# Norm scalars of a batch: the one-column operations on ScalarE instead of VectorE

## The reference

```python
m, s = mean and variance of x over each of 32 groups (4 channels, all pixels)
g = (x - m) / sqrt(s + 1e-5)                      # group norm
u, v = mean and variance (ddof=1) of g over the 128 channels of one pixel
n = (g - u) / (sqrt(v) + 1e-6)                    # per pixel
out = g + g * (W @ n + b)                         # W: 128 x 128, over channels
```

## Time and profile before

| | |
|---|---|
| median of the runs | 1894.35 us (1892.35 to 1896.38) |
| the profiled execution: its own time, its span | 1890.62 us, 1888.8 us |
| mean granted clock of TensorE over the span | 0.996 |
| instructions in the span | 67606 |
| HBM read, written | 394.49 MB, 268.44 MB |
| DMA, mean over the span | 353 GB/s |

### The profile page before, as it was taken

One profiled execution on the slowest core, in us unless ns is written; L12 is line 12 of the kernel. 1 busy time (PEld: TensorE's weight loads), 2 busy tenths in 40 slices (PEclk: granted clock), 3 DMA queues, 4 the chain that ended last, 5 costly groups with the idle time before them and its releaser, 6 DMA issues.

```text
span 1888.8 us, 67606 instructions
## 1 busy us (share of the span) xinstructions
PE 1699.3 (90%) x28706; PEld 920.7 (49%) x28706; DVE 1727.5 (91%) x2120; ACT 1446.4 (77%) x2498; POOL 1458.4 (77%) x1684
## 2 busy tenths in 40 slices
PE   0079998999989999999999999899999999899998
PEld 0045554555545555455555555455545555455553
DVE  5669999999999999999999999999999999988887
ACT  5589886888868986798869889688877898644442
POOL 0068787888878887888878787787877888788885
PEclk9989999999999999999999999999999999999999
DMA  9979999999999999999999999899999999854775
GB/s 375 407 285 375 375 373 327 390 394 391 364 339 406 375 396 342 344 407 382 383 323 393 400 386 381 314 402 386 397 349 340 416 373 397 290 205 189 276 264 221
DMA packets 183036, 667.33 MB, mean 353 GB/s; under 512 B 20560, under 2 KB 20944, under 8 KB 182736
## 3 DMA queue, kind: packets, MB, share of 16 engines
q1 hardware_dynamic: 109008, 394.54, 56.9%
q10 hardware_dynamic: 73728, 268.47, 35.4%
HBM read 394.49 MB, written 268.44 MB: 351 GB/s over the span
## 4 chain that ended last, share of the span: by engine, by line
PE 68%; DVE 18%; issue 6%; DMA 3%; SPq 2%; ACT 2%; POOL 1%; POOLq 0%; ACTq 0%; DVEq 0%
PE proj_ps L731 40%; PE sums_ps L719 15%; PE factor_ps L705 12%; DVE scaled L629 5%; DVE bn L673 4%; DVE bn L674 4%; DMA tiles<-x 3%; SPq L410 2%; DVE tiles L642 1%; DMA out<-tiles 1%; DVE gn L583 1%; ACT unused L511 1%; ACT squares L526 0%; DVE gn L587 0%; POOL tiles L454 0%
## 5 line engine op out<-in xcount | busy, mean ns | idle before, releaser
L731 PE MATMUL proj_ps<-scaled,w_t 128*32 128x512 f32 x8192 | 985.9, 599 | 0.1
L454 POOL TENSOR_SCALAR tiles<-tiles,columns_sb 128x1024 f32<-128x1024 f32 x512 | 576.9, 1127 | 257.4 <-DVE tiles L642 254.4
L642 DVE SCALAR_TENSOR_TENSOR tiles<-proj_ps,columns_sb,tiles 128x1024 f32<-128x1024 f32 x512 | 643.3, 1257 | 69.1 <-PE proj_ps L731 67.5
L511 ACT ACTIVATE unused<-tiles,bn 128x1024 uint8<-128x1024 f32 x560 | 635.2, 1134 | 0.0
L443 POOL TENSOR_SCALAR tiles<-tiles,columns_sb 128x1024 f32<-128x1024 f32 x512 | 620.4, 1212 | 12.9 <-DMA tiles<-x 11.7
L629 DVE TENSOR_TENSOR scaled<-tiles,factor_ps 128x1024 f32<-128x1024 f32 x512 | 619.0, 1209 | 7.2 <-PE factor_ps L705 2.1
L526 ACT ACTIVATE squares<-tiles 128x1024 f32<-128x1024 f32 x512 | 537.8, 1050 | 81.3 <-POOL tiles L443 37.0
L719 PEld LDWEIGHTS sums_ps<-tiles,const_sb 128*32 128x32 f32 x8192 | 245.8, 111 | 316.3 <-issue 265.2
L731 PEld LDWEIGHTS proj_ps<-scaled,w_t 128*32 128x32 f32 x8192 | 213.6, 109 | 360.8 <-issue 306.8
L705 PE MATMUL factor_ps<-pieces,pick_sb 128*128 128x128 bf16 x4096 | 318.1, 221 | 77.2 <-DVE scaled L629 72.5
L719 PE MATMUL sums_ps<-tiles,const_sb 128*32 128x128 f32 x8192 | 320.6, 275 | 11.7 <-ACT squares L526 11.7
(11 more groups left out here) (56 smaller groups left out, 782.3 us busy)
## 6 DMA issues: line engine op xcount, KB each, us to landing
tiles<-x SPq DMA_DIRECT2D x752, 512.0 KB, 8.6
out<-tiles ACTq DMA_DIRECT2D x512, 512.0 KB, 7.1
const_sb<-const SPq DMA_DIRECT2D x1, 85.5 KB, 1.9
scaled<-w SPq DMA_DIRECT2D x1, 64.0 KB, 2.0
scaled<-ident SPq DMA_DIRECT2D x1, 64.0 KB, 1.8
pick_sb<-pick SPq DMA_DIRECT2D x1, 8.0 KB, 2.0
columns_sb<-bias SPq DMA_DIRECT2D x1, 0.5 KB, 2.1
```

Of the source, the lines that this page charges most:

```text
L454: nc.gpsimd.tensor_scalar(place(s), place(s), 1.0, out_shift[:, 0:1], ALU.mult, ALU.add).then_inc(finished, 1)
L511: nc.scalar.activation(unused[:, which, :], data, (ACT.Identity, ACT.Square)[which], bias=pivot_of(of), scale=-1.0, accum_out=act_sums[:, ...
L642: nc.vector.scalar_tensor_tensor(out=place(s), in0=proj_ps[:, s % 2, :], scalar=gate_shift[:, 0:1], in1=place(s), op0=ALU.add, op1=ALU.mul ...
L731: mm = nc.tensor.matmul(proj_ps[q:q + 32, s % 2, h:h + BANK], w_t[:, q:q + 32], scaled[:, s % 2, h:h + BANK], start=True, stop=True)
```

## The change

The `bn_aggr` and the sum of ACT's statistics stay on DVE (`gather`), one step earlier, in step 58. So do the two reciprocals (`invert_root`, `invert_std`). The other small instructions become ACT instructions: eight in `moments` at the end of ACT's step 59, two in `deviation` at the end of step 61, eight in `spread_of_group` in step 62, right behind the square of the slot and ahead of the set work (the pieces of L536 and L539). Each waits for the one before it on `gn_step`, and the sixteenth waits for DVE's reciprocal of the root. PE's two averages stay in steps 61 and 62 (GN_STEP is now 58). DVE's `invert_root` stands in step 62 behind scale, where the clamp stood, and `invert_std` behind the gate of step 62. POOL's wait for slot 0 is for all 18 steps and for `inv_std_done`; the gate of a batch's first slot gets a wait on `gn_step`, which lies nine steps behind. A constant column holds 1e-5.

```diff
-        GN_STEPS = 19
-        GN_STEP = slots - 5
+        GN_STEPS = 18
+        GN_STEP = slots - 6
...
+            def moments(n, of):
+                total = slots * SLOT
+                bn_part = of.bn_slots / slots
+                act.wait_ge(gn_gathered, 2 * n + 2)
+                gn_then(nc.scalar.activation(cell(4), cell(0), ACT.Identity, bias=pivot_of(of), scale=-1.0), n, 1)
+                gn_then(nc.scalar.activation(cell(5), cell(4), ACT.Identity, bias=cell(1), scale=cell(4)), n, 2)
+                gn_then(nc.scalar.activation(cell(6, 2), cell(2, 2), ACT.Copy, scale=1.0 / total), n, 3)
+                gn_then(nc.scalar.activation(cell(8), cell(4), ACT.Identity, bias=cell(6), scale=bn_part), n, 4)
+                gn_then(nc.scalar.activation(cell(9), cell(5), ACT.Identity, bias=cell(7), scale=bn_part), n, 5)
+                gn_then(nc.scalar.activation(cell(10), cell(8), ACT.Copy, scale=-1.0), n, 6)
+                gn_then(nc.scalar.activation(cell(11), cell(8), ACT.Identity, bias=pivot_of(of), scale=-1.0), n, 7)
+                gn_then(nc.scalar.activation(cell(4), cell(8), ACT.Identity, bias=cell(9), scale=cell(10)), n, 8)
+
+            def deviation(n):
+                act.wait_ge(group_mean_done, n + 1)
+                gn_then(nc.scalar.activation(cell(5), small_ps[:, 0:1], ACT.Identity, bias=cell(11), scale=-1.0), n, 9)
+                gn_then(nc.scalar.activation(cell(12), cell(5), ACT.Identity, bias=cell(4), scale=cell(5)), n, 10)
+
+            def spread_of_group(n):
+                act.wait_ge(group_var_done, n + 1)
+                gn_then(nc.scalar.activation(cell(8), small_ps[:, 1:2], ACT.Relu), n, 11)
+                gn_then(nc.scalar.add(cell(9), cell(8), at["gn_eps"]), n, 12)
+                gn_then(nc.scalar.activation(cell(13), cell(9), ACT.Sqrt), n, 13)
+                gn_then(nc.scalar.activation(neg_mean, small_ps[:, 0:1], ACT.Copy, scale=-1.0), n, 14)
...
+                gn_then(nc.scalar.activation(mean, small_ps[:, 0:1], ACT.Copy), n, 15)
+                act.wait_ge(gn_inverse_done, n + 1)
+                gn_then(nc.scalar.activation(cell(10), cell(14), ACT.Identity, bias=cell(13), scale=cell(9)), n, 16)
+                gn_then(nc.scalar.activation(cell(15), cell(10), ACT.Copy, scale=0.5), n, 17)
...
+                gn_then(nc.scalar.activation(gate_new, cell(15), ACT.Identity, bias=bias_sb[:, 0:1]), n, 18)
...
+                    if nxt and step == GN_STEP + 4:
+                        spread_of_group(b + 1)
...
+                    if nxt and step == GN_STEP + 1:
+                        moments(b + 1, of)
                     if nxt and step == GN_STEP + 3:
-                        act.wait_ge(gn_step, (b + 1) * GN_STEPS + 12)
-                        nc.scalar.activation(gn[:, 9:10], gn[:, 8:9], ACT.Sqrt).then_inc(gn_root_done, 1)
+                        deviation(b + 1)
...
+            def gather(n, of):
+                dve.wait_ge(bn_done, bn_before(n) + of.bn_slots)
+                nc.vector.bn_aggr(gn[:, 0:2], bn_of(of)[:, 0:2 * of.bn_slots, :].rearrange("p a b -> p (a b)"))\
+                    .then_inc(gn_gathered, 1)
+                dve.wait_ge(act_done, act_before(n) + 2 * of.act_slots)
+                nc.vector.reduce_sum(gn[:, 2:4], act_sums[:, :, 0:of.act_slots], AXIS_X).then_inc(gn_gathered, 1)
+
+            def invert_root(n):
+                dve.wait_ge(gn_step, n * GN_STEPS + 13)
+                nc.vector.reciprocal(gn[:, 14:15], gn[:, 13:14]).then_inc(gn_inverse_done, 1)
+
+            def invert_std(n):
+                dve.wait_ge(gn_step, n * GN_STEPS + 17)
+                nc.vector.reciprocal(inv_std, gn[:, 15:16]).then_inc(inv_std_done, 1)
...
-                    if nxt and step == GN_STEP + 3:
-                        gn_scalars(b + 1, 2, of)
+                    if nxt and step == GN_STEP + 4:
+                        invert_root(b + 1)
...
-                        gn_scalars(b + 1, 0, of)
-                    if nxt and step == GN_STEP + 2:
-                        gn_scalars(b + 1, 1, of)
-                    if nxt and step == GN_STEP + 3:
-                        gn_scalars(b + 1, 3, of)
+                        gather(b + 1, of)
+                    if nxt and step == GN_STEP + 4:
+                        invert_std(b + 1)
```

More of the change, by code:

```diff
@@ L49 @@
 LOAD_GAP = 0.64
-CONST_COLS = {"group_avg": P, "sum_rows": ROWS + 32, "rows_bc": 1, "rows_c": 1, "norm_eps": 1}
+CONST_COLS = {"group_avg": P, "sum_rows": ROWS + 32, "rows_bc": 1, "rows_c": 1, "norm_eps": 1, "gn_eps": 1}
 def constants(channels):
@@ L69, in constants @@
         "norm_eps": np.full((P, 1), NORM_EPS),
+        "gn_eps": np.full((P, 1), GN_EPS),
     }
@@ L274, in norm_gate_kernel @@
         act_done = sem("act_done")
+        gn_gathered = sem("gn_gathered")
         gn_step = sem("gn_step")
+        gn_inverse_done = sem("gn_inverse_done")
+        inv_std_done = sem("inv_std_done")
         group_mean_done = sem("group_mean_done")
         group_var_done = sem("group_var_done")
-        gn_root_done = sem("gn_root_done")
         norm_scalars_set = sem("norm_scalars_set")
@@ L434, in norm @@
                     pool.wait_ge(gn_step, (batch + 1) * GN_STEPS)
+                    pool.wait_ge(inv_std_done, batch + 1)
                     if own:
@@ L513, in statistics, with cell, gn_then @@
                 del todo[:count]
+            def cell(i, m=1):
+                return gn[:, i:i + m]
+            def gn_then(instruction, n, done):
+                instruction.then_inc(gn_step, 1)
+                act.wait_ge(gn_step, n * GN_STEPS + done)
+            def moments(n, of):
[10 more added lines that the diff above has]
+                gn_then(nc.scalar.activation(cell(4), cell(8), ACT.Identity, bias=cell(9), scale=cell(10)), n, 8)
@@ new lines, in deviation @@
+            def deviation(n):
[8 more added lines that the diff above has]
+                gn_then(nc.scalar.activation(neg_mean, small_ps[:, 0:1], ACT.Copy, scale=-1.0), n, 14)
+                if n > 0:
+                    act.wait_ge(out_shift_set, n)
+                gn_then(nc.scalar.activation(mean, small_ps[:, 0:1], ACT.Copy), n, 15)
+                act.wait_ge(gn_inverse_done, n + 1)
+                gn_then(nc.scalar.activation(cell(10), cell(14), ACT.Identity, bias=cell(13), scale=cell(9)), n, 16)
+                gn_then(nc.scalar.activation(cell(15), cell(10), ACT.Copy, scale=0.5), n, 17)
+                if n > 0:
+                    act.wait_ge(gate_shift_set, n)
+                gn_then(nc.scalar.activation(gate_new, cell(15), ACT.Identity, bias=bias_sb[:, 0:1]), n, 18)
@@ L565, in _ @@
             nc.vector.tensor_copy(w_t[:, :], small_ps[:, 0:P]).then_inc(w_ready, 1)
[L567 to L612, removed]
-                    then(nc.vector.tensor_copy(mean, small_ps[:, 0:1]))
-                    then(nc.vector.tensor_scalar(gate_new, cell(11), bias_sb[:, 0:1], None, ALU.add))
-                    then(nc.vector.reciprocal(inv_std, cell(11)))
-                    assert done[0] == GN_STEPS
@@ L638, in gate @@
                                 dve.wait_ge(gated, b * slots)
+                            dve.wait_ge(gn_step, (b + 1) * GN_STEPS)
                             nc.vector.tensor_copy(gate_shift[:, :], gate_new).then_inc(gate_shift_set, 1)
@@ L736, in period @@
                 for step in steps(own, before, nxt):
-                    if nxt and step == GN_STEP + 2:
-                        pe.wait_ge(gn_step, (b + 1) * GN_STEPS + 9)
+                    if nxt and step == GN_STEP + 3:
+                        pe.wait_ge(gn_step, (b + 1) * GN_STEPS + 8)
                         if own:
                             pe.wait_ge(var_done, b * sets + (sets - 1))
-                        nc.tensor.matmul(small_ps[:, 0:1], at["group_avg"], gn[:, 6:7], start=True, stop=True)\
+                        nc.tensor.matmul(small_ps[:, 0:1], at["group_avg"], gn[:, 11:12], start=True, stop=True)\
                             .then_inc(group_mean_done, 1)
-                    if nxt and step == GN_STEP + 3:
-                        pe.wait_ge(gn_step, (b + 1) * GN_STEPS + 11)
-                        nc.tensor.matmul(small_ps[:, 1:2], at["group_avg"], gn[:, 7:8], start=True, stop=True)\
+                    if nxt and step == GN_STEP + 4:
+                        pe.wait_ge(gn_step, (b + 1) * GN_STEPS + 10)
+                        nc.tensor.matmul(small_ps[:, 1:2], at["group_avg"], gn[:, 12:13], start=True, stop=True)\
                             .then_inc(group_var_done, 1)
```

## The result

The changed kernel took 1875.4 us in the median (1873.71 to 1877.8, 6 runs), beside 1892.77 us for the kernel before (6 runs): ratio 0.9906, 95% interval 0.9894 to 0.9919. That is 17.4 us less, where 10.3 us less had been forecast. The profiled execution took 1875.25 us.

The account below looks back on a forecast made before the run. Boundaries were taken as DVE-bound, the steps around them as PE-bound. From the profiled 1890.6 us: -11.7 - 1.7 - 1.7 + 2.3 + 2.5 = -10.3, 1880.3 us, or 1884 on the runs' scale; range 1878 to 1890, eight in ten 1873 to 1895.

Parts of the forecast that it names:

- Step 59 to 60, "Sum 11.7 us": With part 0 off DVE, PE's spread of step 60 comes sooner at all seven boundaries, 11.7 us less in all.
- The clock, "1.7 us more": At the third boundary the second of two close waits goes, so the granted clock stays up: 1.7 us more gain.
- DMA, "I take a fifth, 2.5 us": Shorter batches find part of their gain back in late loads: a fifth of six times 2.1 us, 2.5 us lost.
- Step 62, T + 5.05: Counted from L746's start, pieces become late next; step 63's spread goes at T + 5.05, 0.25 us sooner, 1.7 us over seven.
- Before batch 0, +2.3 us: Nothing hides ACT's longer chain before batch 0, and a 1.28 us table load falls into it: 2.3 us more.
- Larger gain (1874): The 1.5 us of idle time before step 63 goes too, 10.5 us over seven boundaries: 1874 us, chance 0.10.
- Rivals 3 and 4: Slower: ACT's small step 62 instructions cost more, 1905 us, chance 0.06; or two table loads per boundary, 1904 us, 0.04.
- Rival 2: DMA takes the gain back: loads of steps 54 to 58 keep six of seven batches' length, 1894 us, chance 0.14.

Follow-up runs that it names:

- e5: Changed kernel with only `gather` and `moments` kept; `deviation` and `spread_of_group` left out, that work back on DVE: 1880.07 us, ratio 0.9942 to the kernel before.
- e6: Only the tail of the change: parts 0 and 1 stay on DVE as before, the clamp and all behind it go to ACT: 1890.75 us, ratio 0.999.
- e7: Changed kernel plus 16 one-column DVE instructions without use at the end of step 59 of every batch: 1904.18 us, ratio 1.006 to the kernel before.
- e4: Changed kernel with only the first 512 of each slot's 1024 pixels stored: 1871.22 us, ratio 0.9888 to the kernel before.
- e2: The kernel before, run once more without an edit: 1892.76 us, ratio 0.9999.
- e3: The kernel before with only the first 512 of each slot's 1024 pixels stored: 1892.45 us, ratio 0.9998.

## Why the prediction was wrong in size, point by point

**The mechanism was right.** DVE's part 0 made the hole before step 60, the tail's place on ACT made the pieces the next thing late, and the granted clock stayed at 1.00. e5 and e6 show the two halves, e7 the way back.

**Step 59 to 60, "Sum 11.7 us".** This term was mis-sized. It was the old hole, 14.3 us, less what I let `gather` and late loads cost before step 59, 6.0 us in the changed kernel against 3.4 before. Measured there: 3.8 and 3.1 us, so 13.9 net for the first pair of executions, 13.3 for the second. Two things were off. `gather` costs 1.45, not 1.75 us, and where nothing else is late PE loses 0.07 us to it (e4), not the 0.5 of the first boundary. There I had carried the length of that execution's factor instruction, and at the second and fourth boundary its 1.07 and 1.00 us, into the changed kernel as if they belonged to the place. They move: of the changed kernel's seven only the fourth was of that length, when POOL was in `finish` at the same time.

```profile
954.24 1.12 POOL L458 TENSOR_SCALAR tiles<-tiles,columns_sb 128x1024 f32<-128x1024 f32 x1
...
954.34 1.16 DVE L684 SCALAR_TENSOR_TENSOR sum_sq<-root,approx 128x128 f32<-128x128 f32 x1
```

**The clock, "1.7 us more".** Right in sign, short in number. I took the one fall of one execution for a property of the third boundary and of two waits in a row. It is a chance at each boundary with the hole, higher where the hole is longer: 1, 2, 3 and 1 falls in four executions of kernels with the old hole (before, e2, e3, e6). The median run of before had probably two; that part of the 17.4 us is argued from the profiles and not measured in the timed runs.

**DMA, "I take a fifth, 2.5 us".** This step failed. The loads took nothing of the gain beyond what the boundary's rows had shown already: POOL waits 12.8 and 9.9 us for them after, 11.7 and 10.7 before. The late loads that there are stood already in the step to 59; this term was for a growth of them, a fifth of the most that it could be and read from no row, and nothing grew. What is true of it is another thing: the changed kernel pays 3 us for lateness that the old one's hole covered, and the two kernels with half stores are 21.2 us apart, not 17.4.

**Step 62, T + 5.05.** Measured T + 5.04, at all seven boundaries; the eight instructions took 2.12 us with their waits (308.11 to 310.23), forecast 2.12. Gain 1.85 us, forecast 1.7. **Before batch 0, +2.3 us:** POOL's copy came 10.78 us after the aggregate's start instead of 8.62, +2.16. The Trainium skill's drain (ScalarE: Activation LUTs, What ACT_TABLE_LOAD costs) would have made it 1.4 us more; the Sqrt began 0.01 us after the load (98.22), so no drain shows here. By the Trainium skill (ScalarE: Activation LUTs, Table sets: the hidden batching unit) Relu and Copy are in every set; the trace agrees, with no load in front of either, one between the add and the Sqrt before batch 0 and none at the boundaries. The rule of the Trainium skill (ScalarE: Activation LUTs, Rules for kernel authors) that relu, add and mul belong on VectorE did not hold here: the moved work is some 3 us longer on ACT in all than it was on DVE, and the kernel is 17 us faster.

**The rivals.** Larger gain (1874) came nearest in time, but not by its mechanism: the 1.5 us before step 63 stayed. Rivals 3 and 4 did not occur. Rival 2 did not occur as it was told, by batches that keep their length; what full DMA traffic does take is the 3 us above, and they were in the sum. The sum again, with what was measured (mean of the two pairs): 59 to 60 with 58 to 59 -13.6, clock -2.5, step 62 -1.9, before batch 0 +1.9 (the first spread), loads 0: -16.1; to the last spread the two pairs differ by -15.4 and -17.4.

## What to carry to other kernels

Between two engines that are both busy 90%, look for the stretch where one runs a chain of small instructions alone, and put the chain on an engine that waits there anyway; price it by the instruction and its wait, and name what stands behind it in that engine's program. A chain that lands in front of somebody else's critical instruction gives part of the gain back: its order within the new engine was worth another 10 us. A stall can hide other lateness inside itself, as the old hole hid late loads, and it can bring a cost of its own, as the fall of the clock; so a term for either is read from executions with and without the stall, not from one boundary's rows.

## What was not expected of the hardware

- With 1.8 to 2.9 us of idle time on PE before step 60 the granted clock falls to 0.50 at some boundaries and not at others that look the same, 12 of 35; the step with the fall is 1.5 to 1.7 us longer. After 1.46 to 1.73 us before step 63, and 2.20 us at one boundary of e5, it never fell. What decides between two equal holes stays open.
- DVE's 128x128 factor instruction takes 0.27 to 1.16 us. Where a POOL instruction on 1024 columns had begun 0.1 to 0.9 us before it, it ended 0.13 to 0.15 us after POOL's did (954.24 and 954.34 above: 955.36 and 955.50). Sharing time is not enough: where it began within 0.05 us of POOL's, it took 0.29 us, and POOL's took 1.24 to 1.26 us instead of 1.12 (the changed kernel's first, second, third and fifth boundary). Part 0's L587, on two columns, ended with POOL's instruction in the same way: 0.77 us at the first boundary, to 298.57, where POOL's ended at 298.55, and 0.17 with POOL idle.
- A load planned half a step (1.6 us) sooner lands soon enough to end most waits, although the DMA engines are full for long stretches of a batch.
